# Layer 0's cross attention on one core: value waves in pairs, every fourth step

## The reference, cut to what matters

```python
v = jnp.einsum('nlhd,ed->nlhe', v, Wv)
k = jnp.einsum('nlhd,ed->nlhe', k, Wk)
q = jnp.einsum('nlhd,ed->nlhe', q, Wq)
energy = jnp.einsum('nqhd,nkhd->nhqk', q, k)
energy = jnp.where(mask == 0, jnp.float32(-1e+20), energy)
attention = jax.nn.softmax(energy / jnp.sqrt(jnp.float32(EMBED)), axis=3)
out = jnp.einsum('nhql,nlhd->nqhd', attention, v).reshape(n, q_len, EMBED)
return out @ Wo.T + bo
```

## Time and profile before

| what | value |
|---|---|
| median of three runs | 4505.09 us |
| profiled execution, time / span | 4505.94 / 4503.9 us |
| TensorE busy | 3998.8 us, 89% |
| VectorE busy | 3010.0 us, 67% |
| ScalarE busy | 2216.3 us, 49% |
| GpSimd busy | 1667.3 us, 37% |
| value products, L662, both layers | 4096 instructions, mean 605 to 608 ns |
| score products, L644, both layers | 2048, mean 519 ns |

### The profile page before, as it was taken

The page is one execution under the profiler, slowest core; times in us unless marked ns, Lnnn a source line. Parts: engine busy times, 40 slices in busy tenths (PEclk is TensorE's granted clock), DMA queues, the critical chain, the costliest instruction groups (busy, mean ns, idle before and its releaser), DMA issues. The chain is left out here.

```text
span 4503.9 us, 51238 instructions
## 1 busy us (share of the span) xinstructions
PE 3998.8 (89%) x17936; PEld 2238.5 (50%) x17936; DVE 3010.0 (67%) x3608; ACT 2216.3 (49%) x3355; POOL 1667.3 (37%) x984
## 2 busy tenths in 40 slices
PE   7995899999999686678999779999999988769997
PEld 6883444444444251137777534444444325447775
DVE  3333877777786259945777657777878634467776
ACT  2221466565656333313766416666666631336764
POOL 0001487778778506500000026666666630000000
PEclk9997899999999778979999869999999988789998
DMA  8998566666666300021888636666666540318886
GB/s 308 326 335 274 145 149 149 148 150 148 147 149 145 102 14 0 0 85 64 306 300 303 243 114 153 153 151 152 145 149 146 125 103 9 96 46 309 301 302 229
DMA packets 301551, 751.70 MB, mean 167 GB/s; under 512 B 55793, under 2 KB 89330, under 8 KB 268017
## 3 DMA queue, kind: packets, MB, share of 16 engines
q1 hardware_dynamic: 245136, 560.20, 36.9%
q0 software_dynamic: 47456, 171.46, 18.8%
q10 hardware_dynamic: 8704, 16.78, 1.1%
HBM read 484.23 MB, written 98.37 MB: 129 GB/s over the span
## 5 line engine op out<-in xcount | busy, mean ns | idle before, releaser
L746 ACT ACTIVATE prob<-psum 128x512 f32<-128x512 f32 x1552 | 894.1, 597 | 543.3 <-PE psum L644 498.6
L644 PE MATMUL psum<-q_stack,k_ring 98*128 98x512 f32 x2048 | 1025.2, 519 | 20.0 <-ACT prob L746 14.6
L914 POOL TENSOR_TENSOR den_pool<-den_pool,prob 128x1024 f32<-128x1024 f32 x372 | 935.8, 2516 | 224.0 <-DVE den_pool L826 155.2
L621 PE MATMUL psum<-k_ring,q_stack 96*128 96x512 f32 x2048 | 690.4, 421 | 104.7 <-DMA k_ring<-k_lo 35.6
L797 DVE CUSTOM_DVE_ANT_0 psum<-psum,mask_q 128x1024 f32<-128x1024 f32 x512 | 627.9, 1232 | 222.9 <-PE psum L621 205.4
L793 DVE TENSOR_REDUCE row_max<-psum 128x1 f32<-128x1024 f32 x512 | 614.6, 1219 | 230.8 <-PE psum L621 228.1
L1881 DVE TENSOR_TENSOR weight_lo<-weight_raw,weight_hi 128x2048 fp32r<-128x2048 f32 x240 | 546.9, 2289 | 162.7 <-ACT weight_hi L1824 162.5
L644 PEld LDWEIGHTS psum<-q_stack,k_ring 98*128 98x128 f32 x2048 | 397.9, 195 | 403.1 <-ACT prob L746 275.4
L662 PE MATMUL psum<-prob,x 128*32 128x512 f32 x3104 | 514.7, 608 | 0.9 <-ACT prob L746 0.9
L621 PEld LDWEIGHTS psum<-k_ring,q_stack 96*128 96x128 f32 x2048 | 394.8, 200 | 215.3 <-issue 79.1
L1824 ACT ACTIVATE weight_hi<-weight_raw 128x2048 fp32r<-128x2048 f32 x240 | 453.9, 1915 | 41.7 <-DMA weight_raw<-in_L_ffn_w 22.8
(11 more groups left out here) (421 smaller groups left out, 6362.0 us busy)
## 6 DMA issues: line engine op xcount, KB each, us to landing
weight_raw<-in_L_ffn_w SPq DMA_DIRECT2D x120, 1024.0 KB, 6.4
den_dma<-prob POOLq DMA_DIRECT2D x204, 512.0 KB, 4.9
k_ring<-k_hi SPq DMA_DIRECT2D x1024, 64.0 KB, 2.1
weight_raw<-in_L_ffn_Wu SPq DMA_DIRECT2D x60, 1024.0 KB, 7.1
weight_raw<-in_L_ffn_Wd SPq DMA_DIRECT2D x60, 1024.0 KB, 5.0
den_dma<-xnT POOLq DMA_DIRECT2D x68, 512.0 KB, 4.9
k_ring<-k_lo SPq DMA_DIRECT2D x512, 64.0 KB, 2.4
ctxT<-in_ctxT SPq DMA_DIRECT2D x16, 1024.0 KB, 9.0
```

The lines of the kernel that those rows point to most:

```text
L621: ins = e.matmul(max_banks(q)[:, a * KC:(a + 1) * KC], q_stack[h % n_q][0:QROWS, i * P:(i + 1) * P], k_ring[0:QROWS, (n + a) % kring, :], ...
L644: e.matmul(k.bank(b % 2), k_ring[:, n % kring, kt * P:(kt + 1) * P], q_stack[h % n_q][:], start=not masked, stop=True).then_inc(s_score, 1)
L746: e.activation(prob[b // 2 % n_p][:, b % 2, :], k.bank(b % 2), ACT.Exp, scale=scale).then_inc(s_exp, 1)
L914: e.tensor_tensor(den[:], den[:], tile, ALU.add).then_inc(s_dpool, 1)
```

## The change

`Waves` gets a number `together`. `step` then gives all waves of a group the step of the group's last wave. With `together` = 2 (layer 0) waves 0 and 1 go behind step 4, waves 2 and 3 behind step 8, and so on, waves 14 and 15 behind step 0 of the next head. With `together` = 1 (layer 1) `last` is w itself and nothing changes.

```diff
@@ class Waves
-    def __init__(self, by_pe):
-        self.values, self.sums = [], []
+    def __init__(self, by_pe, together):
+        self.values, self.sums, self.together = [], [], together
@@ class Waves
     def step(self, w):
 
-        return -(-(self.values[w][-1] + 1) // 2)
+        last = min(w - w % self.together + self.together, self.count) - 1
+        return -(-(self.values[last][-1] + 1) // 2)
@@ cross_attention
-    waves = Waves(sums.by_pe)
+    waves = Waves(sums.by_pe, 2 if masked else 1)
```

## The result

The changed kernel takes 4490.91 us in the median of eleven runs (4478.52 to 4498.88), the kernel before 4506.16 in eleven (4501.05 to 4516.28). The ratio is 0.9967 with a 95% interval of 0.9957 to 0.9976, so 15 us faster (11 to 19). 4497 was forecast.

What follows compares the result with a forecast made beforehand. TensorE's own work was taken as the bound in layer 0's cross attention. The terms summed to -8.6 us, -8.1 step by step, from 4505.94 to 4497.8, forecast as 4497 us; 8-in-10 range 4487 to 4508.

Steps and rivals of the forecast that it cites:

- Term 1: Layer 0's 118 wave pairs: a second wave costs 0.86 us instead of 1.08, gaining 0.22 a pair, 26.0 us.
- Term 2: Step 10: the previous head's output loses its neighbouring wave, +0.22 us for 14 heads, +3.1 us; the following wait unchanged.
- Term 3: Handover to the next head: without step 30's wave, TensorE waits 0.47 us for VectorE's remainder; 14 heads, +6.6 us.
- Term 4: VectorE's denominator additions in steps 3 to 6 delay step 8's maxima by 0.19 us; 15 heads, +2.9 us.
- Term 5: Heads 4, 8, 12, reciprocals and multiplications in steps 16 to 23: TensorE waits 1.30 us more a head, +3.9 us.
- Term 6: Last 36 steps, without maxima: four steps take 6.80 us instead of 6.68, +0.9 us in all.
- B: Rival: waits at handover, additions and heads 4, 8, 12 mostly don't come; 4483 to 4491 us; chance 0.11.
- C: Rival: exponentials slow the three successive steps without a wave; at 0.06 us each, 4518 us; chance 0.09.
- D: Rival: the second wave costs 1.08 us like a lone one, so pairs gain nothing; 4521 us; chance 0.04.
- E: Rival: the seven exponential tiles come free too late; a microsecond in half the heads, +8, 4505 us; chance 0.10.

Runs made afterwards that it cites:

- x1_apart: Changed kernel with a pair's two waves put on both sides of the step's second score product; 4519.82 us, 1.0036 of the kernel before.
- x2_short_adds: Kernel before, GpSimd's denominator additions cut from 512 to 8 columns in steps 12 to 25 of heads 4, 8, 12; 4497.69 us.
- x8_after_short: Changed kernel, GpSimd's denominator additions cut from 512 to 8 columns in steps 12 to 25 of heads 4, 8, 12; 4484.58 us.
- x3_handover: Changed kernel with the turned row maxima for the next head one step earlier, at the end of step 28; 4484.97 us.
- x4_head_out: Changed kernel with the previous head's output moved from step 10 to step 12, ahead of that step's pair; 4478.48 us.
- x7_three: Changed kernel with layer 0's waves in threes, every sixth step, instead of pairs; 4490.4 us, 0.9964 of the kernel before.
- x5_both: Changed kernel with the head's output ahead of step 12's pair and the turned maxima at the end of step 28; 4481.04 us.

## Why the prediction was right or wrong

**Bound.** TensorE's own work was the bound: in the ordinary heads the step lengths came out within 0.1 us of the forecast. The stage by terms, forecast and as read from the steps (us, + is longer):

| term | forecast | measured |
|---|---|---|
| 1, 118 pairs | -26.0 | -29.1 |
| 2, head's output | +3.1 | +3.2 |
| 3, handover | +6.6 | +7.0 |
| 4, additions | +2.9 | +4.2 |
| 5, heads 4, 8, 12 | +3.9 | -3.2 |
| 6, last head | +0.9 | +1.35 |
| heads 0 and 14 | not in the sum | about -1.3 |
| sum; the stage | -8.6, step by step -8.1 | -17.9; the stage -18.1 |

**Term 1** was right: 0.86 in the trace, and x1_apart loses 0.23 us a pair step. The pairs gained a little more than the sum had, 0.247 us each instead of 0.22, mostly because the three steps without a wave took 1.39 instead of 1.40. By the Trainium skill's rule that a load only overlaps matmuls of another row group ("TensorE: Matmul & The Clock Gate", packing small matmuls) term 1 would have been nothing. The trace does not agree with it: the second wave's weights load while the first wave runs. (The same section also lets a load go ahead into a background weight buffer; no row tells whether that is so here.) Nor is this peculiar to products of 32 columns: in the kernel before, the weights of a full-width maxima product load at 1188.33 us, while the score product before it runs until 1188.73. The starts show where the 0.22 is paid: a wave starts 0.51 us behind the score product instead of 0.43, its first pass takes 0.02 longer, and the next mask product comes 0.12 later than another wave would. At these edges the loads come only with their products. But so does that of a mask product behind a score product (1188.10), at the usual 0.43 us, so a late load alone need not cost anything. What does cost the 0.22 us no run separates.

**Term 2** was right: step 10 at 2.48, step 11 unchanged at 2.00.

**Term 3** was right in size, 0.46 to 0.47 us a head; there are 15 handovers, not 14. Its explanation was half complete: I had the remainder alone as the cause, and the delayed exponential carries the first 0.22. No run here shows the 0.06 us for the signal before the change; after it the next head's first product follows the remainder by 0.05.

**Term 4** was forecast at 0.19 us and is 0.28 (step 8 at 3.62 against 3.34): the wait is 0.21, and the product behind it takes 0.07 longer, which was not in the sum.

**Term 5** failed. I forecast that TensorE waits 1.3 us longer in each of heads 4, 8 and 12 and took +3.9 us. The waits fell from 1.0, 2.1 and 1.7 to about 0.4, 0.4 and 0.7. The step that failed is the one that kept the four multiplications at the lengths of rows 10. x2_short_adds and x8_after_short show that the long ones are waits behind GpSimd's additions: without these they take 0.29 to 0.30 in the mean. The Trainium skill's lock ("SBUF — State Buffer", who interferes with whom) describes this, and the trace agrees. Shifted by a microsecond, another one is long. This term is 7 of the 10 us between the forecast and the stage. The forecast of the total held, but this term had the wrong direction, and the -3.2 is luck: in x3_handover and x4_head_out, which shift the same operations once more, these heads take 8.1 and 7.0 us more than three ordinary ones, against 1.6 in the changed kernel and 4.8 before.

**Term 6** was forecast at +0.9 us, and the last head is 1.35 us longer.

**Head 0 and head 14** were not in my sum. Head 0 wins 0.8 us in its first step (1.73 against 2.56), but that step varies from kernel to kernel (2.06 to 2.61 elsewhere), so it cannot be counted as a gain of the change. In head 14, step 29 takes 1.98 us instead of 3.00, where the kernel before waited for a copy of 3.1 us.

**Rivals.** B (the waits don't come) was right about term 5 and wrong about 3 and 4. C (exponentials): steps without a wave stand at 1.39, no wait. D: ruled out by x1_apart. E: no ordinary head waits for a tile; once, in step 27 of head 0, ScalarE waits for a denominator DMA and TensorE loses 0.24 us. With threes, ScalarE shows three such waits, 4.0 us in all.

## What to carry to other kernels

Column-tiled products (here 32 columns wide, four side by side in the array) cost least next to each other: the way in and out is paid once a group (0.22 us here), so put every small-column product beside one. Before grouping, ask what each single one had hidden, as the wave of step 30 hid the handover. An operation whose duration in the trace varies tenfold for the same shape is a wait; don't carry its length into a sum, but move it to where a long piece of work covers it. And read the granted clock beside every loss: a loss that looks like missing cover can be a stretch at the lower clock, as in layer 1.

## What the runs showed of the hardware

- The same 128x128 multiplication on VectorE took 0.28 to 3.05 us, and a mean of 0.29 to 0.30 as soon as GpSimd's additions beside it, 2.4 us or more each, were cut. With the long ones, the waits behind them cost a head up to 3.2 us (head 8 of x4_head_out), and more where the clock fell as well. Which head pays changes with any shift of timing.
- After TensorE had waited 2.2 us in x7_three, its granted clock stood at the lower of its two levels for about 7 us, and work of 2.7 us took 4.8. A wait of 1.60 us in x5_both came with such a fall too (a mean of 0.57 from 1035 to 1039 us), while 1.84 us in the kernel before left the clock at 1.00. So the price of a wait is not linear, and not told by its length alone.
- With pairs in layer 1 the lower clock level came up in 11 of 16 heads instead of 3, and a change that wins 0.7 us in a head at full clock lost 14.6 us in all.
- Weights load while products through the same rows still run: for 32-column products from 1022.39 us, with the wave before them busy until 1023.00, and for full-width ones from 1188.33 against 1188.73. Between a full-width product and a wave no load comes ahead (872.28, 874.14 in the changed kernel), and there the 0.22 us is paid.
